# Writing each half of a tile's position rows with a transfer of its own, 64 columns shorter

## The reference

```python
content_score = jnp.einsum('bhsp,bhtp->bhst', q + u, k)
pos_score = jnp.einsum('bhsp,htp->bhst', q + v, pos)
pos_score = _relative_shift(pos_score)      # pad one column left, reshape, drop the first row
score = (content_score + pos_score) / jnp.sqrt(jnp.float32(P))
weights = jax.nn.softmax(score, axis=-1)
out = jnp.einsum('bhst,bhtp->bhsp', weights, val)
```

## Time and profile before

| | us |
|---|---|
| median of 3 runs (lowest, highest) | 9972.04 (9965.46, 9979.7) |
| the profiled execution's own time | 9952.2 |
| its span, first to last instruction | 9950.4 |
| PE busy | 8953.0 |
| DVE busy | 6015.3 |
| ACT busy | 5584.0 |
| POOL busy | 2779.5 |

### The profile page before, as it was taken

How to read it: one execution, slowest core, us unless ns; L and a number is a source line. 1 busy time by engine, 2 the same in 40 slices (tenths; PEclk the granted TensorE clock), 3 DMA queues, 4 the chain that set the end, 5 groups by cost and what they waited for, 6 DMA issues and landing times. The chain is left out here.

```text
span 9950.4 us, 256407 instructions
## 1 busy us (share of the span) xinstructions
PE 8953.0 (90%) x91488; PEld 5835.1 (59%) x91488; DVE 6015.3 (60%) x12530; ACT 5584.0 (56%) x10811; POOL 2779.5 (28%) x2894
## 2 busy tenths in 40 slices
PE   6988999899899899989989989998998999999899
PEld 4666666445566666644556666664555666666445
DVE  4666664664466666467456666646745666663673
ACT  4666664454466666445446666634545666663454
POOL 3333332100333333210033333321003333332101
PEclk8999999899899999989989999998998999999899
DMA  8999994110799999321079999922108999992110
GB/s 311 406 389 394 402 405 163 68 35 24 283 406 397 394 403 398 146 72 33 24 305 404 395 391 406 401 120 73 32 24 329 404 400 394 405 400 97 67 36 24
DMA packets 440127, 2552.03 MB, mean 256 GB/s; under 512 B 60017, under 2 KB 90225, under 8 KB 176369
## 3 DMA queue, kind: packets, MB, share of 16 engines
q1 hardware_dynamic: 438768, 2534.40, 64.6%
HBM read 1284.53 MB, written 1248.85 MB: 255 GB/s over the span
## 5 line engine op out<-in xcount | busy, mean ns | idle before, releaser
L830 POOL TENSOR_SCALAR z<-z,nmax 128x1024 f32<-128x1024 f32 x2048 | 2270.3, 1120 | 3648.5 <-DVE nmax L779 3648.5
L769 DVE CUSTOM_DVE_ANT_0 z<-sc,z 128x1024 f32<-128x1024 f32 x2048 | 2496.2, 1219 | 1182.8 <-DMA z<-rel_rows 1172.3
L726 ACT ACTIVATE rel<-rg 128x512 f32<-128x512 f32 x3072 | 1722.0, 596 | 1590.6 <-PE rg L603 879.8
L731 ACT ACTIVATE pT<-rg 128x512 f32<-128x512 f32 x4096 | 2226.1, 595 | 517.4 <-PE rg L636 516.8
L636 PE MATMUL rg<-ident,z 128*128 128x128 f32 x16384 | 2182.6, 277 | 3.7 <-ACT pT L731 3.2
L636 PEld LDWEIGHTS rg<-ident,z 128*128 128x128 f32 x16384 | 1781.4, 142 | 503.1 <-issue 360.4
L1080 ACT ACTIVATE pT<-rg 128x512 f32<-128x512 f32 (+3 forms) x2560 | 1226.0, 531 | 827.0 <-PE rg L1012 498.0
L1096 DVE TENSOR_REDUCE mx_b<-sc 128x1 f32<-128x1024 f32 (+7 forms) x1024 | 1004.0, 991 | 466.6 <-PE sc L994 231.2
L657 PE MATMUL op<-pT,xnT 128*32 128x128 f32 x32768 | 1121.7, 278 | 4.0 <-DVE rel L808 3.2
L802 DVE COPY rel<-rg 128x512 f32<-128x512 f32 x1024 | 708.4, 692 | 457.0 <-PE rg L607 424.9
L989 PE MATMUL sc<-z 96*128 96x512 bf16 (+3 forms) x2560 | 764.9, 370 | 145.4 <-DMA z<-k_parts 70.0
(11 more groups left out here) (115 smaller groups left out, 8867.1 us busy)
## 6 DMA issues: line engine op xcount, KB each, us to landing
rel_rows<-rel SPq DMA_DIRECT2D x1024, 1088.0 KB, 9.1
z<-rel_rows SPq DMA_DIRECT2D x1024, 1024.0 KB, 9.6
v_heads<-rel SPq DMA_DIRECT2D x8, 4096.0 KB, 12.7
xnT<-v_heads SPq DMA_DIRECT2D x128, 256.0 KB, 4.3
qu_parts<-z SPq DMA_DIRECT2D x36, 512.0 KB, 4.4
pos_s<-pos_parts SPq DMA_DIRECT2D x64, 192.0 KB, 9.4
qv_parts<-z SPq DMA_DIRECT2D x24, 512.0 KB, 7.6
k_parts<-z SPq DMA_DIRECT2D x24, 512.0 KB, 5.2
```

Of the source, the lines that this page charges most:

```text
L726: e.activation(rel[:, r % RING, c * CH:(c + 1) * CH], rg[:, R_BANK[c], :], ACT.Copy).then_inc(r_copied[c], 1)
L731: e.activation(pT[:, t % 2, q * CH:(q + 1) * CH], rg[:, T_BANK[q], :], ACT.Exp, scale=SCALE).then_inc(p_ready[q], 1)
L769: e.tensor_tensor_reduce(out=zs, in0=scf[:, 2 * half * CH:2 * (half + 1) * CH], in1=zs, scale=1.0, scalar=-3.0e38, op0=ALU.add, op1=ALU.ma ...
L830: e.tensor_scalar(zs, zs, 1.0, nmax[:, n % 2:n % 2 + 1], ALU.mult, ALU.add).then_inc(AA[done], 1)
```

## The change

Each tile's write becomes two transfers. The first writes rows 0 to 63 (partitions 0 to 63) without columns 0 to 63; the second writes rows 64 to 127 (partitions 64 to 127) without columns 2112 to 2175. Each moves 64 rows of 2112 float32. Both raise the same semaphore, so a landed tile is now 32 on `rel_out[k]`; the waits of ACT, DVE and SP use the new function `written`, and `Counts` has a field for it. What the reads of `z` fetch is the same as before. The waits ahead of the write move into `rows_ready`, once per tile.

```diff
+SH = P // 2
-Counts = namedtuple("Counts", "tiles fours moves pairs values")
+Counts = namedtuple("Counts", "tiles fours moves pairs values writes")
...
+        def written(base, n):
+
+            return base.writes + 16 * (P // SH) * (n // RING + 1)
...
-                        e.wait_ge(rel_out[r % RING], moved(base, r - RING))
+                        e.wait_ge(rel_out[r % RING], written(base, r - RING))
...
-                e.wait_ge(rel_out[k], e.snap(moved(base, n)))
+                e.wait_ge(rel_out[k], e.snap(written(base, n)))
...
-                there = bass.AP(tensor=rel_d.tensor, offset=hd * FLAT + i0 * W, ap=[[W, P], [1, W]])
-                e.dma_start(there, rel[:, k, :]).then_inc(rel_out[k], 16)
+            def write_rows(n, g):
+
+                k, hd, i0 = n % RING, n // NT % NB, n % NT * P + g * SH
+                c0 = P - SH - g * SH
+                there = bass.AP(tensor=rel_d.tensor, offset=hd * FLAT + i0 * W + c0, ap=[[W, SH], [1, S + SH]])
+                e.dma_start(there, rel[g * SH:(g + 1) * SH, k, c0:c0 + S + SH]).then_inc(rel_out[k], 16)
...
-                    write_rows(base, r)
+                    rows_ready(base, r)
+                    for g in range(P // SH):
+                        write_rows(r, g)
```

More of the change, by code:

```diff
@@ L572, in counts @@
                 return Counts(*(e.snap(b * (nh // HB * per) + p * per)
-                                for per in (G, G // OB, 16 * G // RING, HB // NB * QK_INC, HB // NB * 16)))
+                                for per in (G, G // OB, 16 * G // RING, HB // NB * QK_INC, HB // NB * 16, 16 * (P // SH) * G // RING)))
             with e.Fori(0, 1) as p:
@@ L885, in read_rows, with rows_ready @@
                 e.dma_start(z[:, k, :], shifted).then_inc(rel_in[k], 16)
-            def write_rows(base, n):
-                k, hd, i0 = n % RING, n // NT % NB, n % NT * P
+            def rows_ready(base, n):
                 for c in (R_DVE, R_ACT[-1]):
```

## The result

The changed kernel takes 10,555.48 us (median of 5 runs, 10,478.19 to 10,559.66) against 9972.04 us, a ratio of 1.0566 with a 95% interval of 1.0548 to 1.0585. It is 583 us slower. The prediction was 11,980 us: the direction and the place were right, and the size was 3.4 times too large (2008 us forecast, 583 measured). The measured time lies in the wide range (10,200 to 12,700 us), but outside the likeliest case (11,200 to 12,900 us); it belongs to the rival "the engines fall out of step", which had a chance of 0.12 and named 10,600 us.

The account below looks back on a forecast made before the run. DMA transfers were taken to bound attention A. Confined writes at factor 1.8 add 1.96 us a tile, 2007 us over 1024 tiles; profiled 9952.2 us becomes 11,959, median 11,980 us. Range 10,200 to 12,700 us.

Parts of the forecast that it names:

- the likeliest case: Attention A's half writes take 1.5 to 2.15 times their full-rate time: 11,200 to 12,900 us, chance 0.72.
- the engines fall out of step: Rival: attention A's confined halves complement each other, factor 1.05 to 1.5, 10,020 to 11,200 us, say 10,600; chance 0.12.
- What bounds the stage: In attention A a tile takes as long as its transfers: 5.10 us at 424 GB/s, DMA share 0.99.
- Where the transfers go: Deciding term: each new write reads only half of SBUF's partitions, through fewer doors, 1.96 us more a tile, 2007 us.
- The factor of 1.8: Half writes in attention A take 1.8 times their full-rate time: 4.59 us a tile in place of 2.55.
- The price of a confined byte, from these windows: Step pricing next-head loads in attention A from rate drops: 2.0 times for 48 partitions, 2.1 for 32, 1.5 for 16.
- I take zero for all of this: Extra SP issue, second half's later start, split waits and doubled semaphore count cost nothing; bounds 0 to 0.32 us a tile.
- I am wrong if the rate of calm stretches stays above 400 GB/s: Refuting sign for attention A, where 300 to 320 GB/s was expected in place of 400.
- the sign given for transfers that come late: DMA share under 0.9 while the rate falls too: writes late, not confined; SP or the waits are where to look.
- the case of a sinking clock: Upper part of the likeliest case: idle PE's clock sinks, its 5.2 us a tile passes 7 us, 12,600 to 13,000 us.

Follow-up runs that it names:

- the bare stream: Bare transfers ahead of the kernel before, no engine waiting: eight 1 MB writes and eight reads took 43.0 us whole, 47.4 us in halves.
- the partner: Full-width split with both transfers reading partitions 0 to 63, against the same split with both halves: 11,053.06 us, 487 us more.
- the two runs with GpSimd: Writes issued by GpSimd in place of SP: one write per tile, against the kernel before, 10,164.35 us; full-width halves 10,500.96 us.

## Why the prediction was wrong in size

- **What bounds the stage: right.** The DMA engines do. With the write in one piece a change of their work comes through one for one: the 32,768 bytes a tile were worked out at 79 us and measured at 73.
- **Where the transfers go: right as a mechanism.** 206 GB/s from one half against 418 from the whole, and in even and odd partitions no cost beyond that of a second transfer.
- **The factor of 1.8 failed.** It is the step "The price of a confined byte, from these windows", with the two sentences behind it that a pair of engines in step has nothing that pulls it out, and that the slowest pair decides. Counted as the prediction counts, the changed kernel has a factor of (2.55 + 0.08 + 0.57)/2.55 = 1.25, with every other cost in it. Three things were wrong. The windows overstate the loads' own price: taking their bytes away gave a factor of 1.3 to 1.4, not 2. The loads are also no model of a half: the 48 partitions 0, 2, .. 94 lie in both halves and still came out at 2.0, so the half can't be all that slows them, and what else does stays open. And a slow phase does end: the bare stream with halves goes from 214 to 418 GB/s within some 10 us. Direction adds to it (994 us for the read-back in halves against 596), and so does the partner (487 us).
- **"I take zero for all of this" failed too.** The second transfer costs 70 to 95 us even where it is not confined, inside the bounds of 0 to 0.32 us a tile, but not zero. With halves SP's issues also grow, the write's to 590 ns in the median and the read's to 870, and in the window with a share of 0.88 the DMA engines stand idle part of the time. The two errors have opposite signs.
- **How the 0.58 us a tile of the split divides is open.** The settled stream gives 0.12, the slow start of the bare stream up to 0.55, the two runs with GpSimd at most 0.25 for SP's issues. How often the kernel falls back into the slow phase no run shows; its rate swings between 267 and 417 GB/s in the windows above.
- **The signs.** "I am wrong if the rate of calm stretches stays above 400 GB/s" came true: 417. The stage has about 360 GB/s and 6.13 us between writes where 300 to 320 and 7.6 were expected, and one window fell to a share of 0.88, the sign given for transfers that come late. DVE's wait for `z` was to rise to about 3000 us and rose to 1497, as the smaller loss would suggest. A landing longer than 9.1 us per half was expected, where 7.9 us was measured. PE's granted clock fell a little, from 0.97 to 0.95 or 0.96 in the stage, so the case of a sinking clock did not come.
- **The weights.** The rival that came true stood in the text with the right argument (a partner for the other doors), nearly the right time (10,600 us), and the wrong chance. That the time also fell in the stated range is owed to the range's width.

None of the runs that computes the whole reference beats the kernel before.

## What to carry to other kernels

A stream of transfers that cover only partitions 0 to 63 moves at half rate while the profile's DMA share stays at 1.0, so look at GB/s beside the share, and save bytes in ways that keep all 128 partitions in every transfer (or every second one: even and odd cost 1%). Before you price a term from other transfers in the trace, see that direction, partner and neighbours are the same, and take the bytes away in a run to see whether the price holds. A stretch of bare transfers of each kind gives bounds for the price; cut it into short windows first, since a mean over a start and a settled part is the price of neither of them. And look at the duration of the issues themselves on the queue that issues them: where they grow, everything behind them in that program can come late.

## What the runs showed of the hardware

- Halves in turn gain little into SBUF (219 against 203 GB/s for one half) but much out of SBUF (330 against 206), and with whole reads between them nearly all, after a slow start: 214 GB/s in the first 8 us, 418 from 10 us on, where whole writes have 428.
- An issue on SP takes 320 ns in the median for a write over 128 partitions and at least 445 ns for one over 64, though it has half as many rows. In the kernels with halves single issues on SP take 2 to 3 us; a write's on GpSimd takes 0.74 us at most in its two runs.
- Taking 85.2 MB of loads to 16 to 48 partitions out of a stage bound by transfers saved 262 us, 1.3 times what they would take at 424 GB/s, while windows of 1 to 4 us around their landing had shown 1.5 to 2.1 times.
